# A two-attention, two-FFN block on one Trainium2 core: VectorE's dependent pairs taken apart, a fused offset and maximum, shorter norm offsets, and new orders

## What is computed

```
x = x + attention16(norm(x), ctx)          # 16 heads, 77 keys, softmax
x = x + LN(n + FFN(n)) * gamma + beta,     n = norm(x);  FFN: 256 -> 1024, relu, -> 256
x = x + attention1(LN1(norm(x)), LN2(ctx)) # one head over 77 keys, softmax
x = x + W[idx] @ norm(x) + b[idx]          # idx: the tile of each position, from signed signatures
```

## Time and profile before

| | |
|---|---|
| runs | 273.89, 274.63, 274.74 us |
| profiled execution, span of the core | 272.0 us (no run's own time is listed for it) |
| PE busy | 249.2 us, 92% |
| DVE busy | 220.3 us, 81% |
| POOL busy | 189.7 us, 70% |
| ACT busy | 160.7 us, 59% |
| mean granted clock of PE | 0.982 |

### The profile page before, as it was taken

One profiled execution on the slowest core, in us unless ns is written; L12 is line 12 of the kernel. 1 busy time (PEld: TensorE's weight loads), 2 busy tenths in 40 slices (PEclk: granted clock), 3 DMA queues, 4 the chain that ended last, 5 costly groups with the idle time before them and its releaser, 6 DMA issues.

```text
span 272.0 us, 6214 instructions
## 1 busy us (share of the span) xinstructions
PE 249.2 (92%) x2048; PEld 221.2 (81%) x2048; DVE 220.3 (81%) x573; ACT 160.7 (59%) x510; POOL 189.7 (70%) x361
## 2 busy tenths in 40 slices
PE   1969899899799999999999999999999997989990
PEld 1758676699798879998898799989899996867880
DVE  2899999999998889954999985898587589976551
ACT  3559795864363868695385896457645173465430
POOL 3367788987958896775497788878785497427354
PEclk9995999999999999999999999999999999999997
DMA  6992020011101182000002321121160000000032
GB/s 175 329 326 89 0 81 0 2 39 42 39 2 40 41 265 86 14 9 2 0 2 63 76 77 42 58 60 40 57 217 2 0 0 2 0 2 2 39 154 116
DMA packets 11156, 17.61 MB, mean 65 GB/s; under 512 B 1377, under 2 KB 7509, under 8 KB 11125
## 3 DMA queue, kind: packets, MB, share of 16 engines
q1 hardware_dynamic: 9333, 11.98, 13.9%
q0 software_dynamic: 1792, 5.24, 6.4%
HBM read 14.07 MB, written 3.15 MB: 63 GB/s over the span
## 4 chain that ended last, share of the span: by engine, by line
PE 68%; DVE 15%; POOL 5%; ACT 5%; issue 4%; DMA 1%; SPq 0%; POOLq 0%; DVEq 0%; ACTq 0%
PE PB L266 29%; PE PB L259 12%; PE PB L464 9%; PE S L387 5%; PE PB L339 5%; PE PB L399 4%; PE S L377 4%; ACT E L1066 2%; DVE SX L659 2%; POOL E L1263 1%; DMA WKV<-in_w_k 1%; DVE SX L673 1%; POOL SM L1220 1%; DVE HL L686 1%; DVE XTL L638 1%
## 5 line engine op out<-in xcount | busy, mean ns | idle before, releaser
L1263 POOL TENSOR_TENSOR E<-E,SX 128x308 f32<-128x308 f32 x64 | 43.8, 712 | 10.7 <-DVE SX L676 10.4
L1066 ACT ACTIVATE E<-S,SX 128x77 f32<-128x77 f32 x128 | 39.4, 336 | 10.6 <-DVE SX L659 10.6
L266 PE MATMUL PB<-XTH,W1H 128*128 128x256 f32 x128 | 37.7, 295 | 1.5 <-DVE XTL L638 1.4
L266 PE MATMUL PB<-W2H,HH 128*128 128x256 f32 x128 | 37.6, 294 | 0.0
L266 PE MATMUL PB<-XTL,W1H 128*128 128x256 f32 x128 | 36.2, 283 | 0.0
L266 PE MATMUL PB<-XTH,W1L 128*128 128x256 f32 x128 | 36.2, 282 | 0.0
L266 PE MATMUL PB<-W2H,HL 128*128 128x256 f32 x128 | 35.5, 278 | 0.0
L266 PE MATMUL PB<-W2L,HH 128*128 128x256 f32 x128 | 35.5, 278 | 0.0
L1220 POOL TENSOR_TENSOR SM<-SM,nhalf 128x2 f32<-128x2 f32 x40 | 28.3, 707 | 3.1
L1089 ACT ACTIVATE HH<-PB 128x512 fp32r<-128x512 f32 x32 | 19.0, 598 | 18.0 <-PE PB L266 18.0
L1076 ACT ACTIVATE EW<-S 124x640 f32<-124x640 f32 x32 | 21.9, 711 | 10.9 <-PE S L387 10.1
(11 more groups left out here) (203 smaller groups left out, 725.2 us busy)
## 6 DMA issues: line engine op xcount, KB each, us to landing
RAW<-in_w SPq DMA_DIRECT2D x4, 512.0 KB, 6.3
WD<-in_WD SPq DMA_DIRECT2D x8, 256.0 KB, 4.6
X<-in_x SPq DMA_DIRECT2D x4, 256.0 KB, 5.4
x<-X SPq DMA_DIRECT2D x4, 256.0 KB, 2.1
E<-in_WD SPq DMA_DIRECT2D x4, 256.0 KB
bc<-in_rows SPq DMA_DIRECT2D x1, 640.0 KB, 5.6
X<-in_w1r SPq DMA_DIRECT2D x1, 512.0 KB, 6.6
RT<-in_WD SPq DMA_DIRECT2D x2, 256.0 KB, 2.9
```

Of the source, the lines that this page charges most:

```text
L266: t = e.matmul(dst, a, b, start=first and j == 0, stop=last and j == n - 1)
L1066: t = e.activation(Ei[:, h * NK:(h + 1) * NK], P[:, at:at + NK], ACT.Exp, bias=SX[:, i, 0, k:k + 1], accum_out=SX[:, i, 1, k:k + 1])
L1263: t = e.tensor_tensor(Eh, Eh, SX[:, i, 2, 8 * a + h:8 * a + h + 4].unsqueeze(2).to_broadcast([128, 4, NK]), ALU.mult)
```

## The change

1. `smax` is split into `smax` and `ssub`, `ssum` into `ssum` and `srec`, `x2` into `x2a` and `x2b`, `x3_` into `xr` and `x3_`, and the `r_` calls into single steps. The waits stay, but the list puts other work between the halves. `stats` waits for each half's own first step.
2. `cm` is two fused operations, one per half: scores plus offset, and their minimum. The scores' factor is negated in two places, so the minimum is the negated maximum, and `cex` takes `scale=-1` and waits per half.
3. `rs` for A, C and D makes the offset of one half with one 128x1 operation in place of two 128x2 ones; B keeps the old form.
4. The lists of PE, DVE, ACT and POOL are new, with new PSUM banks.

```diff
-                if apart(g, i, a):
-                    w.wait_ge(s["mx"], n + 1)
...
+            def ssub(g, i, a):
...
+                w.wait_ge(s["mx"], n + 1)
+                if g:
+                    w.wait_ge(s["tE"], n - 3)
...
+            def srec(g, i, a):
...
+                made_here(("sums", n)) if apart(g, i, a) else w.wait_ge(s["ex"], n + 1)
...
+            def x2b(g):
+                Y = dst_of("Y", g)
                 w.wait_ge(s["rsY"], g + 1)
                 w.wait_ge(s["be"], g + 1)
                 for i in range(2):
+                    made_here(("x2a", g, i))
...
             def cm(g):
...
-                e.tensor_tensor(P_, sv, CTB[:, g // 4, :].unsqueeze(1).to_broadcast([128, 2, NK]),
-                                ALU.add).then_inc(s["ca"], 1)
-                w.wait_ge(s["ca"], g + 1)
-                step(e.tensor_reduce(S_[:, 0, :], P_, AX, ALU.max))
-                settle()
-                e.tensor_scalar(S_[:, 1, :], S_[:, 0, :], -1.0, None, ALU.mult).then_inc(s["cm"], 1)
+                for i in range(2):
+                    e.tensor_tensor_reduce(PP[:, i, :], bank("cs", g)[:, i * NK:(i + 1) * NK], CTB[:, g // 4, :], 1.0, BIG,
+                                           ALU.add, ALU.min, accum_out=PS[:, g % 2, 1, i:i + 1]).then_inc(s["cm"], 1)
...
-                if K != "Y":
+                if K in "ACD":
+                    w.wait_ge(s["rs" + K], g + 1)
+                    e.tensor_scalar(smi(K, g, 1, 10, 11), smi(K, g, 1, 6, 7), smi(K, g, 1, 9, 10), -1.0,
+                                    ALU.mult, ALU.mult).then_inc(s["mr" + K], 1)
+                if K == "B":
...
-            r_position(); smax(2, 0, 0); ssum(1, 1, 1); apply("B", 0); smax(2, 0, 1)
...
+            r_position(8); smax(2, 1, 0); ql(3); lo("B", 0); r_index(0); ssum(2, 0, 1); r_index(1); x1(1)
...
```

More of the change, by code:

```diff
@@ L565, in step, with made_here @@
                 steps[0] += 1
+            made = {}
+            def made_here(what):
+                w.wait_ge(s["d"], made[what])
             def settle():
@@ new lines, in vector @@
+            apply("C", 0); srec(3, 1, 0); x1(2); ssum(3, 1, 1); r_pairs(5); srec(3, 1, 1); stats("B", 2)
+            apply("A", 5); ssub(4, 0, 1); r_pairs(6); apply("B", 2); r_pairs(7); lo("A", 5); y(1); stats("A", 6)
+            srec(4, 0, 0); stats("Y", 1); r_pairs(8); x2a(1); ql(5); r_pairs(9); r_pairs(10); smax(4, 1, 0)
+            lo("B", 2); r_pairs(11); r_pairs(12); cm(0); r_bias(0); smax(4, 1, 1); ssum(4, 0, 1); xr(0)
+            srec(4, 0, 1); hl(2, 0); ssub(4, 1, 1); hl(2, 1); x2b(1); srec(4, 1, 0); hl(2, 2); stats("C", 1)
@@ L994, in scalar @@
+            apply("D", 7); pa(1, 0); pa(1, 1); pa(1, 2); pa(1, 3); pa(0, 4); pa(1, 4); pa(0, 5); pa(1, 5); pa(0, 6)
+            pa(1, 6); pa(0, 7); pa(1, 7)
         def scalar(e):
```

455 lines of the change are left out of this document (241 added, 214 removed).

## The result

The changed kernel takes 300.46 us at the median of four runs (298.02 to 301.45); the kernel before took 274.28 in the same job (273.89 to 274.74). The ratio is 1.0938, with an interval of 1.0888 to 1.0989. The profiled execution is the run of 298.02 us, span 296.3 us; the other runs' spans were 297.9, 299.6 and 299.7. Against the 272.0 of before it is 24.3 us longer.

The account below looks back on a forecast made before the run. PE was taken as the bound from 80 to 224 us, with gains possible only at both ends. The terms -5.7 +9.3 +2.3 +2.9 +3.6 -3.0 gave +9.4: span 281.4, time 284.0 us, range 274 to 290 (8 in 10).

Parts of the forecast that it names:

- Term A: First stage: pairs taken apart and PE calls moved forward -6.1, routing in single steps -1.4, late weight load +1.8; -5.7 us.
- Term E: DVE's register loads, now directly ahead of y(6) and lo(B,7) near the end, hold PE: +3.6 us (0 to 5).
- Term C: Store and gather chain around x3_(3): POOL's wait delays rs(Y,4), DVE's x2b(4), then PE; +9.3 us (6 to 12).
- Term F: Tail, 224 to 256 us: earlier pa and pr and split x2 and x3_ close PE's holes; -3.0 us (-4.9 to 0).
- Term D: Half-clock stretch on PE after its 9 us idle at the store and gather chain: +2.3 us (0 to 3).
- Term B: ACT's register loads, now between ex(6,1,1) and et(6,0,0), hold PE: +2.9 us (0 to 4).
- The pair's price: On DVE, a dependent operation right behind its source costs 0.12 us; some 25 pairs before the first FFN make 3 us.
- the rival that pairs cost nothing: DVE starts dependent operations as early as any other, so separating pairs gains nothing: 287.0 us, chance 0.05.
- cm (zero): Second attention's offset and maximum, as fused operations: 0.8 to 1.0 us against 0.89 before, so no effect on time.
- Shorter offsets (zero): POOL's norm offsets, one operation for two, 24 times: 4.8 us less POOL work, zero effect, up to -1 if POOL is late.
- That the starts stay hidden: Rival: register loads on DVE and ACT still cost nothing, the rest holds: 277.5 us, chance 0.14.
- that the chain does not stop PE: Rival: the store and gather chain and its clock loss cost nothing: 272.4 us, or 265.9 with register loads hidden; chance 0.16.

Follow-up runs that it names:

- old_orders_apart: New functions in the previous kernel's orders, with one other call put between the halves of 41 split pairs on DVE: 281.99 us, ratio 1.0253.
- gather_behind: Changed kernel with only POOL's first gather sx(0) moved behind rs(Y,4): 291.36 us, ratio 1.0589 to the kernel before.
- x2b_late: Changed kernel with DVE's x2b(4) and both statistics moved behind ssub(7,1,1), the gather left in place: 300.05 us, ratio 1.0903 to the kernel before.
- act_starts_mid: Changed kernel with only ACT's register loads moved to the middle, ahead of qh(7): 297.2 us, ratio 1.0818 to the kernel before.
- old_then_new_196: New functions, with the previous kernel's lists up to 196 us and the changed kernel's order after: 274.74 us, ratio 1.0004.
- old_orders_starts_late2: New functions in the previous kernel's orders, only DVE's and ACT's register loads moved late, as the change moves them: 280.48 us, ratio 1.0209.
- new_then_old_114: New functions, with the changed kernel's lists to 114 us and the previous kernel's after, ACT's register loads at the seam: 285.55 us, ratio 1.0326.
- three_back: Changed kernel with the gather behind rs(Y,4) and DVE's and ACT's register loads moved to the middle: 285.48 us, ratio 1.041 to the kernel before.

## Why the prediction was right and wrong

The sign and the largest cause were right, the size was not: 9.4 us were forecast in the span, 24.3 came, and the time (284.0 forecast, 300.46 measured) lies above the range. Of the 15.4 us between the forecast and the ledger's 24.8, term A has 7.3, E 3.8, C 2.9, F 1.0, D 0.3 and the small stop that no term had 1.0; B gave 0.9 back. So term A failed by its sign, and E and C were short.

- **Bounds, and which ends can gain.** Right. Between 116 and 224 us the changed lists only lost.
- **Term A (-5.7).** Wrong, and of the wrong sign in the trace: +1.6. The step that failed is "Together 6.1 us of PE work fall into time in which PE stood or waited for DVE". I priced PE's six calls and not what DVE must do first to feed them: ql(3), lo("A", 3), apply("A", 3) and the f_ calls, some 3.4 us, and smax(2, 1, 0) with a reciprocal, 1.0 more. The pairs give back part of it. Up to lo("B", 0) DVE was busy 46.40 us, where it was 43.52, and idle 9.7, where it was 7.9. (The routing up to r_position stands ahead of lo("B", 0) in both kernels and is no part of this.) In a stage where DVE is full, a PE call moved forward takes its DVE calls along. The rows of lo("B", 0), after and then before:

```profile
56.07 0.68 DVE L646 TENSOR_TENSOR XTL<-PB,XTH 128x512 fp32r<-128x512 f32 x1
```

```profile
51.38 0.69 DVE L638 TENSOR_TENSOR XTL<-PB,XTH 128x512 fp32r<-128x512 f32 x1 [0.58 <-ACT XTH L1041]
```

  It comes 4.7 us later: 2.9 of work and 1.8 of idle time. The sign that I gave for this term failed as well. PE was to reach w1(1,0) 5 to 6 us before 72.2 and began it 4.4 us after, though with no idle time before it:

```profile
76.58 0.39 PE L267 MATMUL PB<-XTH,W1H 128*128 128x256 f32 x1
```

  PE had more behind it by then, so the lag at 84 us was still 1.1 us under that of before. That was used up at 106.8 us, where PE waits for DVE again:

```profile
106.83 0.39 PE L267 MATMUL PB<-XTH,W1H 128*128 128x256 f32 x1 [1.42 <-DVE XTL L646]
```

  The w2b load was about right (+1.8 forecast; the lag grew by some 1.5 from 60 to 66 us, and the load landed 3.3 us after ACT could have used it, where 4 was taken), in the chain after:

```profile
52.68 1.80 POOL W1L L1251
...
54.50 3.31 DMA RAW<-in_w
...
57.82 1.06 ACT W2H L1054
```

- **The pair's price (0.12 us).** Confirmed by old_orders_apart, and the rival that pairs cost nothing fell. The Trainium skill says that the semaphore costs nothing extra here ("VectorE: DVE Perf Modes", section "The DRAIN you can't avoid"). Of a wait for the operation just before, the trace disagrees, 73.87 against 72.17 us. But it bought no time in the two kernels that had it alone.
- **cm (zero).** Right in effect, wrong in its price: 0.8 to 1.0 us forecast, 0.40 measured (a call from 174.47 to 174.87). The groups of it after, busy us and mean ns:

```profile
L738 DVE CUSTOM_DVE_ANT_0 PP<-PB,CTB 128x77 f32<-128x77 f32 x16 | 3.1, 231 | 1.8 <-PE PB L260 1.7
L738 DVE DVE_READ_ACCUMULATOR2_ANT PS<- 128x1 f32 x16 | 1.3, 79 | 0.0
```

- **Shorter offsets (zero).** Right in effect. The one operation takes 306 ns where the two took 200 and 227, so 0.1 us is saved each time, not 0.2.
- **Term B (+2.9).** 2.0 us of stop in the profiled execution (the stop itself 1.84), and in gather_behind and x2b_late some 3 more of slow clock. act_starts_mid gives 3.3 of median time for the whole. I gave it no clock: only the stop of 9 us was to bring a slow stretch.
- **Term C (+9.3).** The mechanism was right, link by link, the size short: 12.2. From x3_(3)'s start PE got its go after 18.7 us, where 18.2 were forecast; PE's own list was 9.1, where 8.9 were. The sum lacked one term, in the step "Counted from the end of co(3)". x3_(3) began 2.4 us after co(3) ended (179.48), since DVE had stood 2.52 us at y(4) until 178.11 and had then its backlog to do. 18.7 + 2.4 - 9.1 = 12.0, the stop. "DVE being ahead does not help" was argued; that DVE might be behind was left out.
- **Term D (+2.3).** 2.6 measured: the window from 192 to 208 above, at 0.57.
- **Term E (+3.6).** 7.4. The loads show as 5.68 us of idle time, as forecast. The step that failed is "less co(4) and cs(5), 1.8": PE stopped ahead of cs(5), not behind it, its result's bank being freed by y(6). The DVE and PE rows after:

```profile
236.69 0.69 DVE L710 TENSOR_TENSOR XN<-PB,XN 128x512 f32<-128x512 f32 x1 [5.68 <-issue]
...
237.53 1.96 PE L260 MATMUL PB<-M,XN 128*128 128x77 f32 x8 [4.25 <-DVE XN L710]
```

  And behind this stop too the clock fell, which cost 3.0 of the 7.4:

```profile
236.00:240.00 4.00, 2.47 (x11) 2.50 (x12) 2.54 (x9) 0.19 (x1) 0.00 (x0) 0.64 0.00 0
240.00:244.00 4.00, 4.00 (x21) 4.00 (x20) 2.90 (x10) 1.21 (x5) 2.03 (x5) 0.50 0.00 0
```

- **Term F (-3.0).** -2.0 by the lag, with old_then_new_196 showing much the same in its trace. No time confirms it.
- **The rivals.** None came. That the starts stay hidden is refuted by act_starts_mid and old_orders_starts_late2; that the chain does not stop PE, by gather_behind.

What stays open: how many us the first stage's new order costs as a time. The lag gives +1.6 for one execution and something above zero in all of them, and both kernels that were to measure it were spoilt by their seams. Open too is where the slow stretches lie in the runs that were not profiled.

## What to carry to other kernels

Price a reordering at the waits it moves, with everything queued behind them on every engine: here a call that waited for a chain of store and gather held its own list, and through it the others', for the chain's whole length. A call brought forward brings the calls that feed it along, and where those ran on the full engine nothing was gained. A filler put between two dependent operations must not itself wait: 0.12 us saved stood against 2.3 us lost.

## What was not expected of the hardware

- The clock fell after much shorter stops than the 12 us one: after 4.25 us (0.64 and 0.50 in the two windows above), in gather_behind after 1.83 us of idle time (0.57 and 0.58) and in x2b_late after 2.33 (0.59 and 0.56). In the changed kernel a stop of 1.84 us at the same place left it at 1.00, and in old_orders_starts_late2 one of 2.81 us at 172 us did too. So the same short stop costs 2.9 us more in one execution and nothing more in another.
- The 15 register loads took 5.97 us on DVE and 5.0 to 5.5 us on ACT wherever they stood. They show as 4.1 to 5.9 us of idle time (4.39 on ACT and 5.68 on DVE in the changed kernel, 5.21 in new_then_old_114, 5.92 in three_back), and nothing behind them started.
- The fused addition and minimum on 128x77 takes 231 ns with 79 ns for the accumulator, and overlaps its successor: two halves in 0.40 us, against 0.89 for the three plain operations over both halves.
